# Reordered queues in the expert stage of a gated attention and mixture-of-experts block

## The reference, cut to what matters

```
sim = ctx Wq' Wk ctx' / scale                 # per sequence, 512 x 512, ctx has 128 features
A   = sigmoid(sim) where sim is among the row's 153 largest, else 0;  A = (A + A') / 2
x1  = x + tanh(g0) * ((1 - gamma) * layernorm(x) + gamma * A)

n       = layernorm(x1)                       # 2048 tokens x 512
shared  = silu(n Sg) * (n Su) @ Sd            # Sg, Su: 512 x 256, Sd: 256 x 512
logits  = n R                                 # 8 experts, the top 2, p = sigmoid(logit)
expert  = sum over the two: silu(p n Ge) * (p n Ue) @ De
out     = x1 + tanh(g1) * (shared + expert)
```

## Time and profile before

| | us |
|---|---|
| median of 3 runs (402.62 to 404.21) | 402.77 |
| the profiled execution's own time | 402.77 |
| its span | 401.0 |
| PE busy in the span | 367.5 |
| ACT, DVE, POOL busy | 216.8, 228.9, 134.1 |

### The profile page before, as it was taken

The page is one execution under the profiler, slowest core; times in us unless marked ns, Lnnn a source line. Parts: engine busy times, 40 slices in busy tenths (PEclk is TensorE's granted clock), DMA queues, the critical chain, the costliest instruction groups (busy, mean ns, idle before and its releaser), DMA issues.

```text
span 401.0 us, 6566 instructions
## 1 busy us (share of the span) xinstructions
PE 367.5 (92%) x2018; PEld 202.8 (51%) x2021; DVE 228.9 (57%) x819; ACT 216.8 (54%) x422; POOL 134.1 (33%) x114
## 2 busy tenths in 40 slices
PE   8859889889999999999999999999999999998950
PEld 4314478467755688548955444444444444433310
DVE  1899999998998689852636652332415150505000
ACT  3594877484773696353121475455555647363620
POOL 2201121110534331322303363544536354544231
PEclk9977999999999999999999999999999999999995
DMA  7999971084676542467423444535354454544432
GB/s 215 384 386 382 391 249 13 15 242 130 188 133 184 161 76 32 52 147 172 50 33 79 80 63 97 83 77 107 54 106 66 93 86 78 103 65 96 52 45 33
DMA packets 29353, 51.12 MB, mean 127 GB/s; under 512 B 4614, under 2 KB 7942, under 8 KB 29318
## 3 DMA queue, kind: packets, MB, share of 16 engines
q0 software_dynamic: 9920, 22.16, 32.9%
q1 hardware_dynamic: 19110, 28.40, 20.2%
q10 hardware_dynamic: 288, 0.13, 0.1%
HBM read 28.60 MB, written 22.09 MB: 126 GB/s over the span
## 4 chain that ended last, share of the span: by engine, by line
PE 74%; DMA 9%; DVE 7%; ACT 4%; issue 3%; SPq 1%; POOLq 0%; POOL 0%; DVEq 0%; ACTq 0%
PE gate_up L1292 20%; PE down L1327 15%; PE gate_up L1281 14%; PE gate_up L1288 6%; DMA out_dram<-y_sb,idx 4%; PE turned_x L1263 4%; DMA out_dram<-y_sb,tmp 4%; PE down L1318 3%; PE turned_h L1302 2%; DMA xs<-in_x_dram 2%; PE down L1117 2%; DVE ge_words L1721 2%; PE front L1244 1%; PE front L1155 1%; ACT x L711 1%
## 5 line engine op out<-in xcount | busy, mean ns | idle before, releaser
L1292 PE MATMUL gate_up<-w_gu,xT 128*128 x200 | 89.9, 593 | 0.8 <-DVE hT L2036 0.7
L550 POOL DMA_INDIRECT out_dram<-y_sb,idx x25 | 49.6, 1985 | 73.9 <-DMA out_dram<-y_sb,tmp 26.6
L2031 DVE SCALAR_TENSOR_TENSOR h<-gate_up,p_t,silu 128x256 f32<-128x256 f32 x34 | 16.4, 482 | 80.9 <-ACT silu L745 72.0
L1281 PE MATMUL gate_up<-xT,w_shgu 128*128 128x128 f32 x512 | 59.9, 276 | 1.1 <-ACT xT L722 1.1
L1281 PEld LDWEIGHTS gate_up<-xT,w_shgu 128*128 128x128 f32 x512 | 58.6, 192 | 3.3 <-issue 2.0
L772 ACT ACTIVATE y_sb<-down,gates 128x512 f32<-128x512 f32 x50 | 34.2, 687 | 43.4 <-PE down L1327 28.4
L1292 PEld LDWEIGHTS gate_up<-w_gu,xT 128*128 128x128 f32 x200 | 36.3, 190 | 39.2 <-issue 39.1
L529 POOL DMA_INDIRECT xg<-x_rows,idx x34 | 40.2, 1182 | 36.4 <-DMA x_rows<-payl 15.5
L1327 PE MATMUL down<-w_dn,hT 128*128 x100 | 47.2, 596 | 0.0
L745 ACT ACTIVATE silu<-gate_up,p_t 128x256 f32<-128x256 f32 x34 | 16.1, 473 | 49.1 <-PE gate_up L1292 31.7
L2014 DVE COPY sim<-w_gu 128x2048 f32 x36 | 41.9, 1223 | 0.3 <-issue 0.2
(11 more groups left out here) (222 smaller groups left out, 508.3 us busy)
## 6 DMA issues: line engine op xcount, KB each, us to landing
w_gu<-in_L_ffn_gate_up_w_dram SPq DMA_DIRECT2D x8, 1024.0 KB, 12.2
xs<-in_x_dram SPq DMA_DIRECT2D x4, 1024.0 KB, 6.4
w_dn<-in_L_ffn_down_w_dram SPq DMA_DIRECT2D x8, 512.0 KB, 10.7
out_dram<-xs SPq DMA_DIRECT2D x4, 1024.0 KB, 6.4
x_rows<-x SPq DMA_DIRECT2D x4, 1024.0 KB, 5.1
out_dram<-y_sb POOLq DMA_DIRECT2D x16, 256.0 KB, 4.4
w_gu<-in_ctx_dram SPq DMA_DIRECT2D x4, 256.0 KB, 5.3
xg<-x_rows,idx POOLq DMA_INDIRECT x34, 4.1
```

The lines of the kernel that those rows point to most:

```text
L550: G.indirect_dma_start(out=out[0:2 * N, :] if t < EARLY else out[:, :], out_offset=bass.IndirectOffsetOnAxis(ap=rows, axis=0), in_=y_sb[:, ...
L1281: mm = TE.matmul(g_b[j % 2][:, f * P:(f + 1) * P], w_shgu[:, c, f * P:(f + 1) * P], xT[:, x_slot(j), c], start=(c == 0), stop=(c == DC - 1))
L1292: mm = TE.matmul(g_b[j % 2][:, :], xT[:, x_slot(j), c], w_gu[:, bass.ds(experts[n] * (DC * F2) + c * F2, F2)], start=(c == 0), stop=(c == ...
```

## The change

It moves calls in four lists, takes one group of matmuls away and moves one copy from DVE to ACT. A new helper `stage_up_here(m, g)` on ACT does what `stage_up(m, g)` does on DVE; it is used once, for (8, 3), between `turned_h(46)` and `silu_of(47)`. The semaphore `gu_staged` is raised by both.

- POOL: `gather(9)` and `gather(10)` stand before `scatter(6)` and `shared(19)`, not behind them.
- ACT: `stage_down(0, 1)` comes before `y_of(23)`; `stage_down(8, 2)` and `(8, 3)` come before `silu_of(48)`; `folded_y(46)` comes behind `turned_rows(33)`.
- PE: `warm(5, 6)` ahead of `up(0)` is gone; `up(48)` comes before `fold(46)`.
- DVE: `gate(22)` comes before `read_plan(1)`; `stage_up` calls are mixed with gates and twins in another order; the `weight_of` that followed four `stage_up` calls comes ahead of them, and they are split two and two around the next gate.

```diff
@@ POOL
             scatter(4)
             scatter(5)
+            gather(9)
+            gather(10)
             scatter(6)
             shared(19)
-            gather(9)
-            gather(10)
             shared(20)
@@ ACT
+            def stage_up_here(m, g):
+                act.wait_ge(gu_ps, job_of("M", MIXED[m - 1]) + 1)
+                e = act.value_load(etab_u[0:1, 4 * m + g:4 * m + g + 1], min_val=0, max_val=E - 1)
+                A.copy(unit_gu[:, g], w_gu[:, bass.ds(e * (DC * F2), DC * F2)]).then_inc(gu_staged, 1)
@@
             turned_rows(10)
+            stage_down(0, 1)
             y_of(23)
             y_of(24)
             turned_h(25)
-            stage_down(0, 1)
             stage_down(0, 2)
@@
             turned_h(46)
+            stage_up_here(8, 3)
             silu_of(47)
             turned_rows(32)
             y_of(46)
             turned_h(47)
-            folded_y(46)
             stage_down(8, 0)
             stage_down(8, 1)
+            stage_down(8, 2)
+            stage_down(8, 3)
             silu_of(48)
             turned_rows(33)
+            folded_y(46)
             y_of(47)
             turned_h(48)
-            stage_down(8, 2)
-            stage_down(8, 3)
             silu_of(49)
@@ PE
             pe.wait_ge(sim_ready, 11)
-            warm(5, 6)
             up(0)
@@
             turn_h(47)
+            up(48)
             fold(46)
-            up(48)
             turn_rows(33)
@@ DVE
             place_units()
+            gate(22)
             read_plan(1)
-            gate(22)
             stage_up(0, 0)
+            gate(23)
             stage_up(0, 1)
-            gate(23)
             stage_up(0, 2)
-            stage_up(0, 3)
             gate(24)
             find_twins(0)
+            stage_up(0, 3)
             weight_of(9)
             find_twins(1)
             weight_of(10)
-            find_twins(2)
-            scatter_rows()
             gate(25)
             stage_up(1, 0)
+            find_twins(2)
             stage_up(1, 1)
+            weight_of(11)
+            scatter_rows()
+            gate(26)
+            weight_of(12)
             stage_up(1, 2)
             stage_up(1, 3)
-            weight_of(11)
-            gate(26)
-            weight_of(12)
             gate(27)
             weight_of(13)
             gate(28)
+            weight_of(14)
             stage_up(2, 0)
             stage_up(2, 1)
+            gate(29)
+            weight_of(15)
             stage_up(2, 2)
             stage_up(2, 3)
-            weight_of(14)
-            gate(29)
-            weight_of(15)
             gate(30)
...
             gate(46)
+            weight_of(32)
             stage_up(8, 0)
             stage_up(8, 1)
-            stage_up(8, 2)
-            stage_up(8, 3)
-            weight_of(32)
             gate(47)
             weight_of(33)
+            stage_up(8, 2)
             gate(48)
```

More of the change, by code:

```diff
@@ L2252, in _ @@
             gate(31)
+            weight_of(17)
             stage_up(3, 0)
             stage_up(3, 1)
+            gate(32)
+            weight_of(18)
             stage_up(3, 2)
             stage_up(3, 3)
-            weight_of(17)
-            gate(32)
-            weight_of(18)
             gate(33)
@@ L2262, in _ @@
             gate(34)
+            weight_of(20)
             stage_up(4, 0)
             stage_up(4, 1)
+            gate(35)
+            weight_of(21)
             stage_up(4, 2)
             stage_up(4, 3)
-            weight_of(20)
-            gate(35)
-            weight_of(21)
             gate(36)
@@ L2272, in _ @@
             gate(37)
+            weight_of(23)
             stage_up(5, 0)
             stage_up(5, 1)
+            gate(38)
+            weight_of(24)
             stage_up(5, 2)
             stage_up(5, 3)
-            weight_of(23)
-            gate(38)
-            weight_of(24)
             gate(39)
@@ L2282, in _ @@
             gate(40)
+            weight_of(26)
             stage_up(6, 0)
             stage_up(6, 1)
+            gate(41)
+            weight_of(27)
             stage_up(6, 2)
             stage_up(6, 3)
-            weight_of(26)
-            gate(41)
-            weight_of(27)
             gate(42)
@@ L2292, in _ @@
             gate(43)
+            weight_of(29)
             stage_up(7, 0)
             stage_up(7, 1)
+            gate(44)
+            weight_of(30)
             stage_up(7, 2)
             stage_up(7, 3)
-            weight_of(29)
-            gate(44)
-            weight_of(30)
             gate(45)
```

## The result

The changed kernel takes 413.48 us (median; 411.94 to 414.79) against 402.97 us for the kernel before on the same chip: over all the runs a ratio of 1.0253, with a 95% interval of 1.0207 to 1.0301, so 10.2 us or 2.5% slower (the two medians are 10.5 us apart). 410.8 had been predicted. The profiled execution took 415.18 us with a span of 413.4, 1.7 us above the median.

The account below looks back on a forecast made before the run. PE was taken as the bound, with 74% of the chain and no idle time from 231.4 to 365.2 us. 402.77 + 4.8 (plan) + 0.8 (clock) + 2.4 (end) + 0 + 0 = 410.8 us, range 406.5 to 414.5.

Parts of the forecast that it names:

- Steady part, nothing: DVE's reorder for m = 2 to 7: 0 us, as PE has no idle time; loss at most 1.8 us.
- The plan stage, 4.8 us: Gathers ahead of scatter(6), with a later plan, delay y_of(20) and up(25): 4.8 us lost, bounds 3.6 to 8.4.
- Clock in the plan stage, 0.8 us: PE work at the lower clock after the plan stage's two pauses: 0.8 us lost, between 0 and 1.9.
- warm(5, 6), 0 us: Dropping the matmuls before up(0) costs 0 us, the pause being too short for a clock fall; bound 2.4 us.
- the rival with the front's clock: PE's longer pause before up(0) lowers the clock there: 1.5 us more, 412.3 us; chance 0.16.
- a sign of being wrong: At the front: the granted clock at 0.50 for long after 47 us would show the prediction wrong.
- The end, 2.4 us: up(48) before fold(46) starts no earlier, held by gather(33), so scatter(30) comes 2.4 us later; bounds 1.4 to 4.1.
- Descriptor writing stops while DVE copies: Rival: gather(9), gather(10) and scatter(6) wait out DVE's copies beside them; 1.8 us more, 412.6 us; chance 0.05.
- The plan edit is absorbed: Rival: ACT and PE have other work until scatter(6) lands, only the end costs; 404.9 us; chance 0.10.
- Not slower, paced by the scatters: Rival: scatters, not the fold, pace the end, which comes 1.0 to 1.5 us sooner; 401.0 us; chance 0.07.
- the outer range: Whole kernel: 406.5 to 414.5 us, with under 0.2 chance of falling outside.
- the forecast itself: Whole kernel: the main case against the rivals, 410.8 us likeliest, 408.8 to 413; chance 0.62.

Follow-up runs that it names:

- e7: The kernel before with only DVE's new order for m = 2 to 7; 403.79 us, ratio 0.9999.
- e2: The changed kernel with read_plan(1) ahead of gate(22) on DVE again, POOL's order still changed; 411.88 us, ratio 1.0198.
- e4: The changed kernel with everything for m = 8 as before on PE, ACT and DVE; 410.57 us, ratio 1.0151.
- e8: The changed kernel with stage_up(8, 2) moved ahead of gate(47) and weight_of(33) on DVE; 409.99 us, ratio 1.0158.
- e12: As e11, with folded_y(43) also ahead of turned_rows(30) on ACT; 401.48 us, ratio 0.9947.
- e11: The kernel before with find_twins(2) and scatter rows behind gate(25), DVE's stage_up(8) copies split and the fourth on ACT; 402.66 us, ratio 0.9965.
- e1: The changed kernel with gather(9) and gather(10) back behind scatter(6) and shared(19) on POOL; 409.88 us, ratio 1.0143.

## Why the prediction was right, and where it was off

- *Steady part, nothing.* Right: e7, and 140.00 of 140.00 us of PE in the changed kernel.
- *The plan stage, 4.8 us.* The mechanism was right in each link, and short in one size: the delay of `up(25)` was put at 5.1 us and is 6.1 in the trace, less 0.3 given back, as foreseen. Of this a full microsecond is POOL's issue time. I had 1.7 us from gather to gather and 1.5 for the second; the trace has 1.93 and 2.36, each with its end 0.12 us behind the end of a copy, and `gather(10)` has two copies beside it. `scatter(6)` starts 6.17 us after `gate(22)`, not 5.2. The landing, 4.9 us, is the 4.8 that I took. I had PE's two pauses at 2.5 us each; they are 3.57 and 0.54, since the clock doubled `down(22)` to 3.50 us inside the second.
- *Clock in the plan stage, 0.8 us.* In the changed kernel's trace it is 0: the clock fell after the pause, but came back at 230.5, before `up(25)`. In e2 it fell into `up(25)` and cost 1.7. In e4, whose plan stage is that of the changed kernel, it came back only at 232.7 us, and `up(25)` to `up(48)` took 0.6 us longer; so one trace doesn't say what the timed runs lose here. By the changed kernel's own trace the 0.8 stood in for a loss of clock at another place, and that is luck.
- *warm(5, 6), 0 us.* The step failed in the traces, where the rival with the front's clock came true (1.37 us against its 1.5), and with it a sign of being wrong: the granted clock was 0.50 from 49.6 to 52.9 us. That the pause was shorter than the one of 2.6 us before the old fall was no reason: it was 1.91 us long and a fall followed it in six of seven traces. In timed runs the edit costs 0.4 us, from -0.3 to 1.1, so the 0 stays within what could be measured.
- *The end, 2.4 us.* `up(48)` was held by `gather(33)`, with the old start kept: 14.70 us after `up(46)`, 14.60 before. Order and waits made 2.7 of the 4.4 us in the trace; the other 1.7 is the low clock in `up(48)`, which I had only in the bound. The term should have carried it: a pause of 2.3 us stood in my own working, and 2.43 was measured.
- *Descriptor writing stops while DVE copies.* I gave this rival 0.05, and its mechanism is what the traces show; its price in the plan stage was 1.1 us (1.93 less 1.7 and 2.36 less 1.5), not 1.8, since `scatter(6)` met no copy. The row of 2.87 us, which I held against it, was misread. These are the third of the four copies beside that scatter, and the first of the two beside `gather(10)`, both in the kernel before:

```profile
326.51 1.23 DVE L2014 COPY sim<-w_gu 128x2048 f32 x1
213.22 1.27 DVE L2014 COPY sim<-w_gu 128x2048 f32 x1 [0.19 <-issue]
```

  The scatter ended at 327.83, 0.09 us behind the end of its copy, and the gather at 214.61, 0.12 us behind. A block that ends with each single copy lets an issue finish between four copies; the last section has the count.
- *The plan edit is absorbed.* No: ACT stood for 10.17 us and PE's two pauses came.
- *Not slower, paced by the scatters.* No: POOL was idle for 8.76 us before `scatter(30)`. e8 meets its condition, an early `up(48)`, and still only gets back to the old end, since `folded_y(46)` then comes after a whole `up`.

The sum came out 2.2 us low by the ratio (10.2 measured, 8.0 predicted). In the trace the two stages account for it: 1.0 us of POOL issue in the plan stage, 1.7 of clock and 0.3 of order at the end, less the 0.8 of clock that I put in the wrong place. The front's 1.37 us is in the trace beside these and hardly in the timed runs. The result lies well inside the outer range, but at the upper edge of the 408.8 to 413 of the forecast itself, and nearer to the sums of two rivals (412.3 and 412.6) than to 410.8, so the number alone would not have decided between them; the traces had to. The low bound of the plan stage adds up to 3.8 us, not 3.6, which changes nothing here.

## What to carry to other kernels

Before a call is moved up on an in-order queue, name what it waits for and what then stands behind it: here two gathers that waited for a plan took a scatter, a buffer, ACT and PE with them, and the same edit cost 1.8 us alone and 4.4 in the changed kernel, where the plan was late too. A pause on PE has to be priced with the clock after it, and PE's filled stretches tell which reorderings can be left alone. Where the end is a serial row of DMAs, start its first link early and keep other engines' copies away from their issue.

## What was not expected of the hardware

- The issue of an indirect DMA on POOL goes by the ends of DVE's copies. In the fourteen traces 338 gathers and scatters overlap a `stage_up` copy on DVE, and 331 of them end at one of three distances behind the end of a copy: 0.08 to 0.12 us (191), 0.88 to 0.89 us (133 gathers, of 1.01 us when alone) or 1.48 to 1.50 us (7 scatters, of 1.58 us when alone). So how long an issue takes depends on where in a copy it starts. `gather(10)` started 0.01 us after a copy in the kernel before, took 1.38 us and was done 0.12 us behind that copy; in the changed kernel it started 0.11 us after one, took 2.36 us and was done 0.12 us behind the next. `scatter(28)` took 3.33 to 3.43 us beside four copies in one piece and was done with the last, 2.20 to 2.45 where they are split or fewer, and 1.92 in e12. The copies pay too: 1.42 us beside a scatter at the end of the changed kernel, 1.22 alone. The Trainium skill's page SBUF — State Buffer, section "SBUF: two separate sides", calls the port pair that VectorE and GpSimd share an exclusive lock for the whole instruction, with the other fully blocked. The traces agree, if the lock is given over between one copy and the next; no run was made to test this alone.
- Each fall of the clock inside PE's work here, between `up(0)` and its last matmul, followed a pause: 1.9 us before `up(0)` (in six of seven traces), 2.2 before `up(25)` in e2, 3.6 before `down(22)`, 2.4 before `up(48)`. A pause of 1.6 us near 80 us stands in all fourteen traces, and a fall at 82 us followed it in two, e7 and e11. Pauses of 1.3 us before `fold(46)` in the kernel before and in e4 were followed by none, nor was e1's of 1.5 before `up(25)`.
